# Layer 1's feed-forward: two of its tiles beside the last attention quarters, and layer 2's first quarters beside the other six

## The reference, cut to what matters

```python
x = x + _L1_xattn_ref(_layernorm(x), ctx, ...)      # 16 heads of 16, int8 rows in and out
x = x + _L1_ffn_ref(_layernorm(x), w1, b1, w2, b2)
x = x + _L2_attn_ref(_layernorm(x), Wq, Wk, Wv, Wo) # 32 query heads of 8, causal

def _bitlinear(x, w, b):
    xn = _layer_norm(x)
    xq = _activation_quant(xn)        # int8 grid by each row's maximum
    return einsum('bsd,fd->bsf', xq, _weight_quant(w)) + b
h = _bitlinear(x, w1, b1)             # 256 -> 1024
h = gelu(h, approximate=False)
return _bitlinear(h, w2, b2)          # 1024 -> 256
```

## Time and profile before

| | us |
|---|---|
| median of 3 runs | 2355.17 |
| lowest, highest | 2354.26, 2366.03 |
| the profiled execution | 2366.2 |
| its span | 2364.2 |
| PE busy in the span | 2013.3 (85%) |
| DVE, ACT, POOL busy | 1570.7, 1152.7, 855.5 |
| the chain that ended last: PE, DVE, ACT | 69%, 13%, 7% |

### The profile page before, as it was taken

How to read it: one execution, slowest core, us unless ns; L and a number is a source line. 1 busy time by engine, 2 the same in 40 slices (tenths; PEclk the granted TensorE clock), 3 DMA queues, 4 the chain that set the end, 5 groups by cost and what they waited for, 6 DMA issues and landing times.

```text
span 2364.2 us, 38315 instructions
## 1 busy us (share of the span) xinstructions
PE 2013.3 (85%) x13443; PEld 1456.4 (62%) x13521; DVE 1570.7 (66%) x4123; ACT 1152.7 (49%) x2563; POOL 855.5 (36%) x1374
## 2 busy tenths in 40 slices
PE   5999967899985799955698999589999999997991
PEld 4888844566652456532255667368788787774670
DVE  4876657456668456546577979578888888765433
ACT  1347647334438344426557646155555655552330
POOL 3248751112123111110000000166766767764445
PEclk9999978999996699975699999799999999998996
DMA  6114430000000300010000000411111111135543
GB/s 262 44 66 145 146 127 1 1 2 2 2 30 0 148 8 2 2 38 1 0 1 1 1 1 1 158 41 41 49 51 46 41 41 46 45 104 161 122 134 104
DMA packets 57693, 130.96 MB, mean 55 GB/s; under 512 B 6656, under 2 KB 23552, under 8 KB 55520
## 3 DMA queue, kind: packets, MB, share of 16 engines
q1 hardware_dynamic: 52656, 115.80, 14.3%
q0 software_dynamic: 4560, 12.46, 2.5%
q10 hardware_dynamic: 288, 0.26, 0.0%
HBM read 100.31 MB, written 26.08 MB: 53 GB/s over the span
## 4 chain that ended last, share of the span: by engine, by line
PE 69%; DVE 13%; ACT 7%; issue 4%; POOL 4%; DMA 1%; SPq 1%; POOLq 0%; another core or an unknown queue 0%; DVEq 0%; ACTq 0%
PE ps L1072 4%; PE ps L2690 4%; PE ps L2349 4%; PE ps L2368 4%; PE ps L2712 3%; PE ps L2736 3%; PE ps L1112 3%; PE ps L3144 3%; PE ps L1092 3%; PE ps L1139 2%; PE ps L2744 2%; PE ps L2681 2%; PE ps L2672 2%; PE ps L2673 2%; PE ps L601 2%
## 5 line engine op out<-in xcount | busy, mean ns | idle before, releaser
L3000 POOL TENSOR_TENSOR K<-K 128x512 f32<-128x512 f32 x128 | 144.8, 1131 | 146.8 <-DVE K L2797 146.8
L2397 DVE TENSOR_TENSOR_SCAN W<-W,ps 128x512 f32<-128x512 f32 x128 | 155.8, 1218 | 40.1 <-issue 24.6
L1305 ACT ACTIVATE K<-ps 128x768 f32<-128x768 f32 (+1 forms) x128 | 110.7, 865 | 146.2 <-PE ps L1112 144.5
L2349 PEld LDWEIGHTS ps<-K 128*128 128x128 f32 x1024 | 136.6, 196 | 65.0 <-issue 50.6
L2940 ACT ACTIVATE K<-ps,K 128x256 f32<-128x256 f32 x128 | 60.8, 475 | 213.8 <-DVE K L2781 213.8
L2792 DVE TENSOR_SCALAR K<-ps,K 128x128 f32<-128x128 f32 x384 | 131.0, 404 | 27.5 <-POOL K L3017 27.1
L2349 PE MATMUL ps<-K 128*128 128x128 f32 x1024 | 139.2, 280 | 6.8 <-DVE W L2397 6.8
L2986 POOL TENSOR_SCALAR K<-K 128x1 f32<-128x1 f32 x16 | 3.6, 224 | 371.3 <-DVE K L2847 368.9
L237 POOL TENSOR_SCALAR Z<-Z 128x1 f32<-128x1 f32 x80 | 19.9, 248 | 321.6 <-DVE Z L232 321.6
L2368 PE MATMUL ps<-W,C 128*128 128x512 f32 x256 | 132.2, 598 | 0.7 <-DVE W L2405 0.6
L2690 PE MATMUL ps<-K 128*128 128x256 f32 x512 | 131.8, 380 | 0.7 <-ACT K L2959 0.7
(11 more groups left out here) (523 smaller groups left out, 5748.1 us busy)
## 6 DMA issues: line engine op xcount, KB each, us to landing
W<-split_weights SPq DMA_DIRECT2D x32, 768.0 KB, 4.3
split_weights<-W SPq DMA_DIRECT2D x40, 384.0 KB, 2.6
W<-in_m SPq DMA_DIRECT2D x32, 256.0 KB, 4.8
results<-K SPq DMA_DIRECT2D x63, 128.0 KB
W<-split_weights SPq DMA_DIRECT2D x1, 5376.0 KB, 16.6
W<-in_wproj SPq DMA_DIRECT2D x16, 256.0 KB, 3.1
W<-in_m SPq DMA_DIRECT2D x32, 128.0 KB, 5.1
W<-split_weights SPq DMA_DIRECT2D x1, 3072.0 KB, 21.0
```

What stands on the lines that cost most here:

```text
L1305: e.activation(to, made, ACT.Exp, scale=self.SCALE).then_inc(*self.up("exp"))
L2349: m = e.matmul(ps[1 + 2 * (n % 2)][:, b * 128:(b + 1) * 128], self.dtuT[h][:, i, b * 128:(b + 1) * 128], self.diag[s % 4][:, b * 128:(b + ...
L2397: e.tensor_tensor_scan(self.st[i % 3], self.a[i % 3], ps[1 + 2 * (i % 2)][:, :], 0.0, ALU.mult, ALU.add).then_inc(*sig.up("m scan"))
L3000: e.tensor_tensor(Pv, Pv, st[:, 4:6].unsqueeze(2).to_broadcast([128, 2, 256]), ALU.mult).then_inc(*sig.up("x scaled"))
```

## The change: what it does

Tiles 0 and 1 of the feed-forward start at steps 0 and 2 and run through all their phases beside the heads' quarters 104 to 130 (`EARLY` now begins at quarter 104, with a step after every second quarter). Their products lie in banks 5 and 6, which the heads' last projection units have left. Tiles 2 to 5 start at steps 12 to 15, tiles 6 and 7 at steps 19 and 20 (`FROM`), their products in banks 2, 3, 4 and 7. There are 32 steps in place of 21; 19 of them (0 to 18) stand before the heads' end, in place of 7. From step 15 on, each step is followed by two of layer 2's quarters, as long as these are below -1. All waits that guard the shared banks and areas are rewritten for this, and `am, ax` move to another area of memory.

```diff
     def __init__(self, g, heads):
...
-    PHASES = 14
+    PHASES, FIRST = 14, 2
+    FROM = (0, 2, 12, 13, 14, 15, 19, 20)
...
-    STEPS = NT + PHASES - 1
+    STEPS = FROM[-1] + PHASES - 2
     def tiles(self, step):
-        return [(t, step - t) for t in range(max(0, step - self.PHASES + 1), min(NT, step + 1))]
+        return [(t, step - self.FROM[t]) for t in range(NT) if 0 <= step - self.FROM[t] < self.PHASES]
+    def reached(self, ph, step):
+        return sum(start + ph <= step for start in self.FROM)
+    def bank(self, tile, n):
+        return self.ps[((5, 6, 5, 6, 5, 6) if tile < self.FIRST else (4, 2, 3, 7, 4, 7))[n]]
...
         for i, ph in self.tiles(step):
+            if ph in (2, 3, 6, 7, 11) and i < self.FIRST:
+                for u in range(len(h.last) - 2, len(h.last)):
+                    h.wait_part(t, u, h.last[u])
+                t.wait_ge(sig["l1f kept"], self.reached(2, step - 1))
+                t.wait_ge(sig["l1f biased"], 2 * self.reached(3, step - 1))
+                t.wait_ge(sig["l1f hidden kept"], self.reached(6, step - 1))
+                t.wait_ge(sig["l1f x"], self.reached(7, step - 1))
+                t.wait_ge(sig[nx.name + " xnT"], nx.tbase + self.reached(11, step - 1))
             if ph == 2:
                 t.wait_ge(sig["l1f rows"], i + 1)
                 t.wait_ge(sig["l1f kept"], i)
-                t.wait_ge(self.heads.s("exp"), 2 * self.heads.N)
-                pb = ps[2].bitcast(BF16)
+                if i >= self.FIRST:
+                    t.wait_ge(h.s("quad kept"), h.N)
+                    t.wait_ge(sig["l1f x"], self.reached(7, step))
+                pb = self.bank(i, 0).bitcast(BF16)
...
-    EARLY = {124: 0, 126: 1, 129: 2, 132: 3, 136: 4, 140: 5, 145: 6}
-    BESIDE, CROSS = 12, 18
+    EARLY = {104: 0, 106: 1, 108: 2, 110: 3, 112: 4, 114: 5, 116: 6, 118: 7, 120: 8, 122: 9, 124: 10, 126: 11, 128: 12,
+             130: 13, 131: 14, 133: 15, 136: 16, 139: 17, 143: 18}
+    BESIDE, CROSS = 15, 18
...
             yield "heads", q
             if q in self.EARLY:
-                yield "ffn", self.EARLY[q]
-        first, behind = max(self.EARLY.values()) + 1, list(self.attn.quarters)
-        for step in range(first, self.ffn.STEPS):
-            yield "ffn", step
-            if step >= self.BESIDE:
-                for q in behind[3 * (step - self.BESIDE):3 * (step - self.BESIDE) + 3]:
-                    yield "attn", q
-        for q in behind[3 * (self.ffn.STEPS - self.BESIDE):]:
+                yield from self.beside(self.EARLY[q], behind)
+        for step in range(max(self.EARLY.values()) + 1, self.ffn.STEPS):
+            yield from self.beside(step, behind)
+        for q in behind:
             yield "attn", q
+    def beside(self, step, behind):
+        yield "ffn", step
+        for n in range(2):
+            if step >= self.BESIDE and behind[0] < -1:
+                yield "attn", behind.pop(0)
...
     def banks_free(self, t, q):
-        if q >= -4 * self.attn.LEAD:
+        if q >= -1:
             t.wait_ge(self.sig["l1f biased"], 2 * NT)
-        if q >= -1:
             t.wait_ge(self.sig["l1f kept"], NT)
```

More of the change, by code:

```diff
@@ L1409, in __init__ @@
         self.quantised = Area(g.W, 3200, 4096).ring(2, 256)
[L1410 removed]
+        self.am, self.ax = late.new(NT, 3), late.new(NT, 3)
         self.Q = [[a.new(4, 256, dt=BF16) for _ in range(2)] for _ in range(self.SETS)]
@@ L1575, in pe_at @@
                 t.wait_ge(sig["l1f x"], i)
-                t.wait_ge(self.heads.s("quad kept"), self.heads.N)
+                t.wait_ge(sig["l1f kept"], self.reached(2, step - 1))
                 for j in range(8):
-                    m = e.matmul(ps[4][:, 0:256], self.rgT[i % 3][:, j, :], self.w2[:, j, :], start=j == 0, stop=j == 7)
+                    m = e.matmul(self.bank(i, 4)[:, 0:256], self.rgT[i % 3][:, j, :], self.w2[:, j, :], start=j == 0, stop=j == 7)
                 m.then_inc(*sig.up("l1f out"))
             elif ph == 11:
-                t.wait_ge(self.heads.s("kept"), len(self.heads.number))
-                g.norms[6].turn(t, i, ps[7])
+                t.wait_ge(sig["l1f hidden kept"], self.reached(6, step - 1))
+                nx.turn(t, i, self.bank(i, 5))
     def dve_at(self, v, step):
-        g, sig, ps, e = self.g, self.sig, self.ps, v.e
+        g, sig, e = self.g, self.sig, v.e
         xn = g.norms[5].xn
@@ L1795, in order @@
                     yield "heads", q
+        behind = [q for q in self.attn.quarters]
         for q in front[3 * (self.cross.STEPS - self.CROSS):]:
@@ L1820, in cross_read, with heads_read @@
             eng.wait_ge(sig["l0f rows"], NT)
-    def heads_ended(self, eng):
+    def heads_read(self, eng, q):
         h, nx = self.heads, self.g.norms[5]
[L1825 to L1829, removed]
-        eng.wait_ge(h.s("exp"), 2 * h.N)
-        eng.wait_ge(h.s("unit"), len(h.made))
-        eng.wait_ge(h.s("parts"), h.N // 2)
-        eng.wait_ge(h.s("quantised"), NT)
-        eng.wait_ge(self.sig[nx.name + " xn"], nx.base + NT)
+        if q == self.attn.quarters[0]:
+            eng.wait_ge(h.s("logits"), 2 * h.N)
+            eng.wait_ge(h.s("unit"), len(h.made))
+            eng.wait_ge(h.s("maximum"), 2 * h.N)
+            eng.wait_ge(h.s("parts"), h.N // 2)
+        if q == 0:
+            eng.wait_ge(h.s("rest"), max(h.made_rest.values()))
+            eng.wait_ge(h.s("kept"), len(h.number))
+            eng.wait_ge(h.s("quads"), h.N)
+            eng.wait_ge(h.s("quad kept"), h.N)
+            eng.wait_ge(h.s("quantised"), NT)
+            eng.wait_ge(self.sig[nx.name + " xn"], nx.base + NT)
     def cross_banks(self, t, q):
@@ L1871, in pe @@
             elif stage == "ffn":
+                t.wait_ge(self.heads.s("unit"), len(self.heads.made))
                 self.ffn.pe_at(t, n)
             else:
-                if n == self.attn.quarters[0]:
-                    self.heads_ended(t)
+                self.heads_read(t, n)
                 self.banks_free(t, n)
@@ L1889, in dve @@
             elif stage == "ffn":
+                v.wait_ge(self.heads.s("unit"), len(self.heads.made))
                 self.ffn.dve_at(v, n)
             else:
+                self.heads_read(v, n)
                 if n == self.attn.quarters[0]:
-                    self.heads_ended(v)
                     self.attn.dve_begin(v)
```

34 lines of the change are left out of this document (20 added, 14 removed).

## The result

| | before | after |
|---|---|---|
| median of four runs each, side by side | 2360.6 | 2398.1 |
| lowest, highest | 2354.3, 2366.8 | 2393.7, 2400.4 |
| the profiled execution, its span | 2366.2, 2364.2 | 2393.7, 2391.8 |
| part A (quarter 107 to 127) | 28.4 | 70.8 |
| part B (quarter 127 to quarter -1) | 110.1 | 102.0 |

The ratio after to before is 1.0157 (95% interval 1.0118 to 1.0196): 28 to 46 us slower, where 19 to 20 were forecast (2375 against 2355). Part B is what was forecast, 102 us. Part A was to grow by 27 us and grew by 42. The two parts together grew by 34.3 us, the profiled executions by 27.5: quarter 107 starts at 665.87 us in the one after and at 672.26 in the one before, though nothing is changed ahead of it. A and B are free of this.

A forecast was written before the change was run, and what follows sets the result against it. PE was taken to bound the heads, DVE and ACT the feed-forward's middle. Part A +27 and part B -8 gave +19 on the median of 2355.2, so 2375; the forecast's own range 2365 to 2386, the whole range 2350 to 2393.

The forecast's parts named there:

- Part B: Quarter 127 to layer 2's quarter -1: six tiles instead of eight, layer 2's quarters inside; 102 for 110.1 us, -8.
- Part A: two tiles enter the loop: Up to quarter 127: two tiles' work enters the loop of PE and ACT; 24.2 us at full clock, 27 with clock.
- The clock: Part A: idle PE slows six probability groups and their values on the chain; 0 to 6 us, 3 taken.
- Phases 0 and 1 at quarters 104 and 106, where DVE has 4.6 of 20 us free, 0.7: Part A: these two phases, placed where DVE has idle time, add 0.7 us, within the rest of +2.2.
- The chain from quarter 111 to 117: Part A: bias, Gelu groups, loads, exponentials and phase 5 in order take 22.2 us in place of 7.1; +15.1.
- From 117 to 121: Part A: heads' work, output addition, tile 1's phase 5 and the exponential take 11.5 us for 5.6; +5.9.
- Table loads: Six loads in the stretch in place of two, 1.28 us each; the skill's figure would make A 4 us dearer.
- The ring: Part B: with two quarters behind a step, PE, DVE and ACT wait in a circle; 10.0 us per full step.
- The first item: Part B: from quarter 127 to the first unit's copy, steps 12 to 15; 17.5 us.
- The faster one: Both parts: B at 85 us, -25, and A costing only its work, 12; total 2342; chance 0.11.
- the even one: Both parts: A +27 as forecast, B at DVE's floor, -25; +2, total 2357; chance 0.22.
- The third: PE at 1.2 GHz through A and B: A's clock term +6, B 112, layer 2's start 5; +37, 2392; chance 0.12.

The follow-up runs named there:

- e1: Changed kernel with POOL's maxima parts of quarters 104 and 112 moved behind steps 0 and 4: part A 64.8 (70.8 after), total 1.0078 of before.
- e6: e1 with 24 added 128x512 products on PE beside steps 6 and 8: part A 61.8 against 64.8, total 1.0094 of before.
- e2: Changed kernel with Identity in place of the Gelu of tiles 0 and 1, two table loads instead of six: part A 66.3, total 1.0092 of before.
- e3: Changed kernel with the edits of e1 and e2 together: part A 59.3, part B 102.3, total 1.0059 of before.
- e9: e1 with DVE's phase 5 of tiles 0 and 1 two quarters earlier, and their Gelu left out: part A 47.7 (51.2 with the Gelu).
- e4: Changed kernel with layer 2's quarters -24 to -2 all behind the feed-forward's last step: part A 71.7, part B 109.2, total 1.0153 of before.
- e10: e7 with six added products on constants behind quarter 119 on PE: part A 28.5, part B 108.7, total 0.9975 of before.
- e12: e10 plus three added products behind each of layer 2's quarters -21 to -2: part A 28.5, part B 110.2, total 0.9966 of before.
- e7: Kernel before with phases 0 and 1 of tile 0 and phase 0 of tile 1 beside quarters 117 and 119: part A 33.2, total 0.9984 of before.
- e15: e7 profiled a second time with no edit: part A 33.1, part B 107.8.
- e13: The kernel before, profiled a second time with no edit: part A 26.9, part B 110.5.

## Why the prediction was right in direction and wrong in size

**The failed step: "Part A: two tiles enter the loop", the sum 24.2 + 3 = 27, which measured about 41.** The mechanism, a loop of PE and ACT that pays for what is put between, was right in the main, and three of its terms were too small.

- *POOL's queue, 0 taken, 6 to 7 measured* (e1). For part A the prediction named PE, DVE and ACT in order and what is queued behind each, and for SP that its loads cost nothing. It gave no reason for leaving POOL out of the sum, and said nothing of what stands ahead of a moved step there. The instruction itself is 0.55 us; it was ten others ahead of it, waiting for DVE's maxima of the heads, that made it late. While the steps stood behind quarter 124, after the last scores, there were no such parts to wait for.
- *The clock, 3 taken, about 10 read from the trace.* "0 to 6" was bounded by six probability groups and their values. The longer products, the scores between and the output projections are on the chain too. Since before loses 0 to 6 us there itself, 3.4 over its four profiles, the growth that belongs to the clock is nearer 7. e6 gave 3 us of it back and the rest was not taken away by an experiment.
- *"Phases 0 and 1 at quarters 104 and 106, where DVE has 4.6 of 20 us free, 0.7".* With POOL's order mended (e1), the step from quarter 107 to 109 takes 5.04 us where before had 2.85: 2.2 us. A share of idle time over 20 us said that there was room, but on DVE and on ACT the rows stand ahead of the heads' next exponential. The first paragraph says itself that whatever ACT waits for between two exponentials goes into the loop.

These give 24.2 + 6.0 + 6.6 + 1.5 = 38.3 of the 41 (6.6 is the clock's 10 less the 3.4 of before, 1.5 the rows' 2.2 less 0.7), or 39.3 with 7.0 for POOL. Where the last 2 to 3 us lie is open.

**The chain from quarter 111 to 117, forecast 22.2 at full clock,** is right in its rows. It took 28.8; e1 shows 3.4 of the difference to be POOL, and three groups at 1.2 GHz ahead of the second wait (1.89, 1.94 and 1.46) are 2.3 more. From 117 to 121 it was 11.5 forecast, 13.9 measured, with PE at 1.2 GHz behind its wait at 711.93 (1.89 us, and its values as long).

**Table loads, 1.28 each.** Measured so in every profile, with the next activation 1.29 us behind a load's start where its input was ready; four loads taken away gave 3.5 to 5.5 us (e2, e3, e9), where the prediction had three on the chain, 3.8. The Trainium skill ("ScalarE: Activation LUTs", "What ACT_TABLE_LOAD costs") gives 2.66 us for a switch; three would be 8.0, as an estimate from that figure, and no run shows it. The Trainium skill advises in the section "Table sets" of the same page to batch activations by set. The runs agree that the added switches cost time: 4.5 of 41 us (e2), where the order around them is 20.

**Part B, 102 forecast, 102.0 and 100.5 measured.** The ring was the right picture: in the profile after, the unit's products that close three rings in a row (L1057 at 782.48, 791.60 and 801.36) lie 9.1 and 9.8 us apart, forecast 10.0, and without quarters beside the steps B is 109.2 (e4). The first item's terms add up to 17.3, where the prediction writes 17.5. The units' products at less than full clock cost 4.0 us over their 1.89 each, of the 5 taken for them and the first products.

**Rivals.** The faster one and the even one needed part B at 85, and it never was. The third had PE at 1.2 GHz through A and B, 37 us slower, 2392. Measured was 1.57%, or 37 us, but that it came out is luck: its A was 30 for 41 and its B 112 for 102. The clock's 10 us in A and POOL's 6 took the place of B's 10.

**What would have shown it beforehand.** The same ten instructions stand in the trace of the kernel before, in its timeline of POOL, 1.1 us behind the start of quarter 107's probabilities (672.26):

```profile
673.35 0.22 POOL L1350 CAST K<-K 128x8 bf16<-128x8 f32 x1 [13.80 <-issue]
...
675.51 0.22 POOL L1360 CAST K<-K 128x8 bf16<-128x8 f32 x1
```

The order of the changed kernel tells that they stand ahead of L1709. The two together show the queue; its length is the 2.4 us from 673.35 to 675.73.

## What to carry to other kernels

When a step is moved in kernels with a fixed order on each engine, ask of every instruction in it, however small, what stands *ahead* of it on its engine and what that waits for; a free share of an engine says nothing on this. Where two engines hand work back and forth, what is put between is paid for together with what it waits for, and the place of the same instructions can be half of the price (20 of 41 us here). Before a few microseconds of one profile are explained by an edit, profile the unedited kernel again: here one stretch of one program took 26.9 or 33.0 us by PE's clock alone. And compare profiles at an equal clock, or a real price (1.6 us for the moved rows) is lost in it.

## What the runs showed that I had not expected

- After the same idle time of 1.43 us, in the same program at the same instruction, PE went on at 2.4 GHz in two profiles (in one of them it fell right behind the first group of probabilities, for some 3 us) and at 1.2 GHz in two others (1.89 us for each group of probabilities in place of 1.05).
- Products on constants whose result nobody reads, 1.5 us of them, stood in both profiles of that order that kept the clock (e10, e12; without them it fell in both, e7 and e15), and 60 of them ahead of quarter -1 brought 7.0 us back behind it: PE had been busy 9.4 and 9.9 of 10 us at a granted clock of 0.50 and 0.55 for 20 us. Since the clock also holds by chance at the first place (e13), two profiles with and two without don't show that such products always keep it.
